# An LSTM with a feed-forward network: up to three GpSimd operations in a time step in place of two, and a new order of the work around them

## What is computed

```python
xW = einsum('ntd,dg->ntg', x, Wx) + b          # x: 32 x 64 x 256, Wx: 256 x 1024
def step(carry, xw_t):
    a = xw_t + prev_h @ Wh                     # 32 x 256 @ 256 x 1024
    i, f, o = sigmoid(...); g = tanh(a[:, 3*Hd:])
    next_c = f * prev_c + i * g
    next_h = o * tanh(next_c)
h = concatenate([hs, -hs], -1)
h = s0 * (h @ sign(k0));  h = relu(h) * 2      # to 1024 features
h = s1 * (h @ sign(k1));  h = relu(h) * 2      # 1024 x 1024
y = x + s2 * (h @ sign(k2))                    # to 256
```

## Time and profile before

| | |
|---|---|
| median of three runs | 273.42 us (273.35 to 273.68) |
| the profiled execution | 273.12 us, of which its span is 271.3 us |
| PE busy in the span | 264.2 us, 97% |
| DVE, ACT, POOL busy | 223.3, 190.7 and 83.1 us |
| chain that ended last | 80% PE, 10% DVE, 3% ACT |
| granted TensorE clock | 1.0 |

### The profile page before, as it was taken

The page is one execution under the profiler, slowest core; times in us unless marked ns, Lnnn a source line. Parts: engine busy times, 40 slices in busy tenths (PEclk is TensorE's granted clock), DMA queues, the critical chain, the costliest instruction groups (busy, mean ns, idle before and its releaser), DMA issues.

```text
span 271.3 us, 8591 instructions
## 1 busy us (share of the span) xinstructions
PE 264.2 (97%) x3360; PEld 196.1 (72%) x3360; DVE 223.3 (82%) x833; ACT 190.7 (70%) x597; POOL 83.1 (31%) x115
## 2 busy tenths in 40 slices
PE   8999999999999999899999999999999999999996
PEld 5777878888898898788988988755666544444444
DVE  3798888899898889988798999887869499993573
ACT  4798887888977778888898778888855478323220
POOL 0030200133344534533443522433422184040220
DMA  6980000000000000000000000000001010000004
GB/s 184 363 350 2 2 2 0 2 4 2 4 2 1 6 0 2 2 5 2 2 2 2 4 17 25 2 2 4 2 23 39 22 40 0 1 2 0 0 0 155
DMA packets 5288, 8.71 MB, mean 32 GB/s; under 512 B 640, under 2 KB 2944, under 8 KB 5120
## 3 DMA queue, kind: packets, MB, share of 16 engines
q1 hardware_dynamic: 4960, 7.64, 8.1%
q10 hardware_dynamic: 288, 0.52, 0.5%
HBM read 6.07 MB, written 2.10 MB: 30 GB/s over the span
## 4 chain that ended last, share of the span: by engine, by line
PE 80%; DVE 10%; ACT 3%; DMA 2%; issue 2%; POOL 1%; SPq 1%; DVEq 0%; POOLq 0%
PE WK L750 16%; PE WK L811 13%; PE WK L733 10%; PE WK L792 7%; PE GFO L712 5%; PE G L703 4%; PE G L712 4%; PE GFO L703 4%; PE ACC L834 4%; DVE aT L1346 3%; PE G L811 3%; PE GFO L852 3%; DMA xw<-in_wx 2%; PE WK L852 2%; PE WK L770 1%
## 5 line engine op out<-in xcount | busy, mean ns | idle before, releaser
L971 ACT ACTIVATE tT<-aT 128x64 f32<-128x64 f32 x189 | 44.9, 269 | 27.1 <-DVE aT L1346 19.4
L750 PE MATMUL WK<-h,k 128*128 128x256 f16 (+1 forms) x408 | 59.4, 287 | 0.1
L1346 DVE TENSOR_REDUCE aT<-GFO 128x64 f32<-128x128 f32 x128 | 36.5, 285 | 11.7 <-PE GFO L712 10.0
L750 PEld LDWEIGHTS WK<-h,k 128*128 128x128 fp8e5 x408 | 37.8, 98 | 8.8 <-ACT xw L954 0.2
L733 PE MATMUL WK<-xs,wxs 128*128 128x512 f32 x168 | 43.4, 402 | 0.0
L712 PE MATMUL GFO<-h,w 128*128 128x64 f16 x504 | 35.1, 192 | 0.0
L733 PEld LDWEIGHTS WK<-xs,wxs 128*128 128x128 f32 x168 | 30.1, 188 | 6.4 <-DVE xs L1179 0.4
L703 PEld LDWEIGHTS G<-h,w 128*128 128x128 f16 x504 | 17.8, 96 | 14.1 <-DVE h L1458 10.7
L1346 DVE TENSOR_REDUCE aT<-G 128x128 f32<-128x256 f32 x64 | 27.1, 424 | 0.0
L712 PE MATMUL G<-h,w 128*128 128x64 f16 x504 | 25.0, 193 | 0.0
L703 PE MATMUL G<-h,w 128*128 128x32 f16 x504 | 22.9, 178 | 1.7 <-DVE h L1458 1.5
(11 more groups left out here) (193 smaller groups left out, 538.8 us busy)
## 6 DMA issues: line engine op xcount, KB each, us to landing
x<-in_x SPq DMA_DIRECT2D x3, 512.0 KB, 8.1
xw<-in_wh SPq DMA_DIRECT2D x4, 256.0 KB, 5.9
k<-in_k SPq DMA_DIRECT2D x1, 1024.0 KB, 10.0
out_y<-x SPq DMA_DIRECT2D x8, 128.0 KB, 1.8
out_y<-x SPq DMA_DIRECT2D x3, 256.0 KB, 2.1
x<-in_x ACTq DMA_DIRECT2D x2, 256.0 KB, 3.6
xw<-in_wx SPq DMA_DIRECT2D x4, 128.0 KB, 4.4
xw<-in_wx SPq DMA_DIRECT2D x2, 256.0 KB, 6.1
```

The lines of the kernel that those rows point to most:

```text
L750: ins = eng.matmul(layer_src(tile), w, rhs, start=a == 0, stop=last)
L971: eng.activation(tT[:, B * j0:B * j1], aT[:, j0:j1].rearrange("p j b -> p (j b)"), ACT.Tanh, scale=half_gain0 if t == 0 else half_gain).th ...
L1346: eng.tensor_reduce(aT[:, j0:j1], G[g][:, 0:64 * (j1 - j0)].rearrange("p (j h b) -> p j b h", h=2, b=B), op=ALU.add, axis=AX.X).then_inc(a ...
```

## The change

- `CHORES` goes from 1.3 to 2.0. So POOL's list for a step can hold three operations of 0.65.
- DVE makes 16 parts of `mix` (0 to 7 and 16 to 23) and POOL 16. Such a part may now also stand in `dve[t]`, behind h.
- In place of `fresh` the planner has `late`: for each operation of ACT and POOL the time in the next step's PE work at which it is taken as done. PE's matmuls that need it, or need the PSUM bank that it frees, are put behind that point.
- A product with `mix` waits only for its own eight parts, by the semaphores `mixed0`, `mixed1` and `mixed3`.
- The first layer of chunk 4 may start with step 48, without the added delay of one step a tile.
- `ORDER` is another string.

```diff
-MIX_ORDER = tuple(range(16, 24)) + tuple(range(8, 16)) + tuple(range(24, 32))
-VECTOR_MIXES = 8
-CHORES, WINDOW, LOOK = 1.3, 1.25, 24
+MIX_ORDER = tuple(range(8, 16)) + tuple(range(24, 32))
+VECTOR_MIXES = tuple(range(8)) + tuple(range(16, 24))
+CHORES, WINDOW, LOOK = 2.0, 1.25, 24
...
+    def free_at(tile):
+
+        if tile is None:
+            return 0.0
+        ops = by_whom(tile)
+        return max(late.get(op, 0.0) for op in ops) if made.issuperset(ops) else T
...
         def have(*ops):
-            return made.issuperset(ops) and fresh.isdisjoint(ops)
+            return made.issuperset(ops) and all(late.get(op, 0.0) <= now for op in ops)
...
         elif q == 0:
-            inputs = t >= sum(CHUNKS[tile[1]]) + (tile[2] if tile[1] == N1 else 0)
+            inputs = t >= sum(CHUNKS[tile[1]])
...
-        return inputs and (old is None or emptied(old))
+        return inputs and free_at(old) <= now
...
+            now = spent if t < 0 or t > 16 else 0.9
             at = choose(t)
...
             if t == MIX_STEP:
-                to_dve += [(("mix", n), [], t) for n in range(8)]
+                to_dve += [(("mix", n), [], t) for n in VECTOR_MIXES]
...
-                if since <= t and op[0] not in pair + ("cl", "mix", "tl", "th") and (made | first).issuperset(needs) and len(dve[t]) < room:
+                if since <= t and op[0] not in pair + ("cl", "tl", "th") and (made | first).issuperset(needs) and len(dve[t]) < room:
...
-        fresh = {("P", op) for op in pool[t][1:]}
+        late = {}
+        for n, op in enumerate(act[t]):
+            late["A", op] = sum(map(act_cost, act[t][:n + 1])) - 0.9
+        for n, op in enumerate(pool[t]):
+            late["P", op] = sum(map(pool_cost, pool[t][:n + 1])) - 0.49 + 0.02 * n
...
                 elif q == 3:
-                    e.wait_ge(mixed, len(MIX_ORDER))
+                    e.wait_ge(mixed3, 8)
                     e.wait_ge(lo22S, k + 1)
                 else:
                     i = (3, 0, 1, 2)[q - 4]
-                    e.wait_ge(mixed0, VECTOR_MIXES)
-                    e.wait_ge(mixed, len(MIX_ORDER))
+                    if q in (5, 7):
+                        e.wait_ge(mixed0, 8 if q == 5 else len(VECTOR_MIXES))
+                    elif q == 6:
+                        e.wait_ge(mixed1, 8)
...
+                q, k, cols = n // 8, n % 8 // 2, slice(256 * (n % 2), 256 * (n % 2) + 256)
+                u, v, op = (a21, a22, ALU.add) if q == 0 else (a11, a21, ALU.subtract)
                 e.wait_ge(w1_made, 3)
-                eng.tensor_tensor(mix[:, 0, k, cols], a21[:, k, cols], a22[:, k, cols], ALU.add, saturate=False).then_inc(mixed0)
+                eng.tensor_tensor(mix[:, q, k, cols], u[:, k, cols], v[:, k, cols], op, saturate=False).then_inc(mixed0)
```

More of the change, by code:

```diff
@@ L190, in make_plan @@
     made = {("A", ("x", 0, j)) for j in range(NJ)}
-    fresh = set()
+    late, now = {}, 0.0
     to_act, to_dve, to_pool = [], [], []
@@ L210, in emptied @@
             ops = [("V", tile)]
-        return made.issuperset(ops)
+        return ops
     def ready(tile, a, t):
         def have(*ops):
-            return made.issuperset(ops) and fresh.isdisjoint(ops)
+            return made.issuperset(ops) and all(late.get(op, 0.0) <= now for op in ops)
         q, k = tile[0], a % 8 // 2
-        mixed = [("P", ("mix", n)) for n in MIX_ORDER]
+        mixed = {q: [("V" if n < 8 or 16 <= n < 24 else "P", ("mix", n)) for n in range(8 * i, 8 * i + 8)]
+                 for i, q in enumerate(("s5", "s6", "s7", "s3"))}
         if q == "x":
@@ L229, in ready @@
         elif q == "s3":
-            inputs = have(("V", ("l22", k)), *mixed)
+            inputs = have(("V", ("l22", k)), *mixed[q])
         elif q[0] == "s":
-            inputs = have(by("tl", {"s4": 3, "s5": 0, "s6": 1, "s7": 2}[q], k), *mixed)
+            inputs = have(by("tl", {"s4": 3, "s5": 0, "s6": 1, "s7": 2}[q], k), *mixed.get(q, ()))
         elif q in ("p1", "p2"):
@@ L254, in ready @@
         else:
-            return inputs and any(emptied(old) for _, old in free)
-        return inputs and (old is None or emptied(old))
+            return inputs and any(free_at(old) <= now for _, old in free)
+        return inputs and free_at(old) <= now
     def place(tile):
@@ L264, in place @@
         else:
-            bank[tile], before[tile] = free.pop(next((n for n, (_, old) in enumerate(free) if emptied(old)), 0))
+            bank[tile], before[tile] = free.pop(next((n for n, (_, old) in enumerate(free) if free_at(old) <= now), 0))
     def after(tile):
@@ L572, in lstm_ffn @@
         acc_mm, y_out, y_made = ([sem(f"{n}{mo}") for mo in range(2)] for n in ("acc_mm", "y_out", "y_made"))
-        mixed, mixed0, p1_made, n2_mm, r12_made, hi22, lo22 = (
-            sem(n) for n in ("mixed", "mixed0", "p1_made", "n2_mm", "r12_made", "hi22", "lo22"))
+        mixed0, mixed1, mixed3, p1_made, n2_mm, r12_made, hi22, lo22 = (
+            sem(n) for n in ("mixed0", "mixed1", "mixed3", "p1_made", "n2_mm", "r12_made", "hi22", "lo22"))
         rest_made, rest_lo = ({c: sem(f"{n}{c}") for c in (SA, N1 - 1, N1)} for n in ("rest_made", "rest_lo"))
@@ L1278, in empty @@
                 elif op[0] == "mix":
-                    mix0_part(op[1])
+                    own_mix_part(op[1])
                 elif op[0] == "t":
@@ L1522, in _ @@
                 x_hi(2, k)
-            mix_order = [op[1] for ops in pool_plan for op in ops if op[0] == "mix"]
             def mix_part(n):
                 q, k, cols = n // 8, n % 8 // 2, slice(256 * (n % 2), 256 * (n % 2) + 256)
-                u, v, op = ((mix[:, 0], a11, ALU.subtract), (a11, a21, ALU.subtract), (a12, mix[:, 1], ALU.subtract))[q - 1]
+                u, v = (mix[:, 0], a11) if q == 1 else (a12, mix[:, 1])
                 eng.wait_ge(w1_made, 3)
@@ L1532, in mix_part @@
                     eng.wait_ge(mixed0, n - 8 + 1)
-                elif q == 3:
-                    eng.wait_ge(mixed, mix_order.index(n - 16) + 1)
-                eng.tensor_tensor(mix[:, q, k, cols], u[:, k, cols], v[:, k, cols], op, saturate=False).then_inc(mixed)
+                else:
+                    eng.wait_ge(mixed1, n - 24 + 1)
+                eng.tensor_tensor(mix[:, q, k, cols], u[:, k, cols], v[:, k, cols], ALU.subtract, saturate=False).then_inc(mixed1 if q == 1 else mixed3)
             def s_term(i, k):
```

13 lines of the change are left out of this document (6 added, 7 removed).

## The result

The changed kernel takes 274.28 us in the median (273.38 to 275.02), the kernel before beside it 273.35 (272.74 to 273.78). The ratio is 1.0036, with an interval of 1.0025 to 1.0046. So it is slower, by 0.9 us. The profiled execution took 274.63 with a span of 272.8; the one of before took 273.12.

What follows compares the result with a forecast made beforehand. With 18 matmuls a step, PE's work and the chain through DVE and ACT were taken as equally long, 2.85 us. Terms -3.3 - 1.2 + 6.1 = +1.6, put on the median 273.42, gave 275.0, range 273.8 to 276.9.

Steps and rivals of the forecast that it cites:

- The two gains: Shorter steps through PE's new order and fewer waits, -3.3 us, and fewer matmuls in the tail, -1.2 us.
- What the change gives back in the steps: Steps 16 to 63: evener matmul order and fewer PE waits for POOL cut the excess from 4.47 to 1.2, -3.3.
- the twelve: Steps 14, 17 to 21, 29, 31, 33, 34, 36, 37, where POOL gets three operations; forecast 3.2 to 3.5 each.
- The tail: After h of step 63: 578 matmuls in place of 589, 11 less at 0.109, -1.2 us.
- The price of the third operation: POOL's third operation holds vT until 0.08 behind its end, in twelve steps, 0.39 to 0.65 each: +6.1 us.
- The 0.04 for the hand-over to uT and back: In each step with three POOL operations, 0.04 us allowed for passing the turn to uT and back.
- `mix` on DVE behind h pushes POOL: Steps 17, 20 and 21: a part of `mix` on DVE delays POOL's first operation, 0.2 more each.
- The bounds: Limits on the third operation's price: 5.1 with no hand-over or push, 7.3 with hand-over 0.1 and push 0.26.
- Faster, vT gets its turn at once: Rival: POOL's third operation doesn't hold the chain, as vT and cD are too short or go at once; 268.9, chance 0.13.
- No change, 0.35 a step: Rival: DVE's operations take the port ahead of POOL more often, 12 times 0.35 is 4.2, to 273.1; chance 0.07.
- Slower still: Rival: several hand-overs a step and PE readers too early, 12 times 0.7, 277.3; chance 0.10, shared with waits that stay.
- the order does nothing: Rival: PE's waits in steps 55, 59 and 61 stay (2.1), 277.1 with the holding; chance 0.10, shared with slower still.

Runs made afterwards that it cites:

- the first run: The changed kernel with CHORES back from 2.0 to 1.4, so at most two POOL operations a step, PE's and DVE's rows unchanged: 269.52 us against 272.98 before.
- both runs without the holding: The changed kernel with CHORES 1.4 (269.52 us), and the changed kernel with each third POOL operation replaced by a memset (269.1 us).
- the first two experiments: The changed kernel with CHORES 1.4 (ratio 0.9879 to the kernel before), and with a memset as third POOL operation in twelve steps (ratio 0.9867).

## Why the prediction was right, and where its terms were off

The sign, the mechanism and the size hold: 275.0 forecast, 274.28 measured, +1.6 against +0.9. In the profiled pair the sum comes nearer (+1.51) than its terms deserve. Counted as the prediction counts it, the price of the third operation is 5.4 (5.13 in eleven steps, 0.31 in step 14), 0.7 under the 6.1. The two gains were 0.15 and 0.11 short, and 0.36 at the start, which no term had, gave back the rest.

- **What the change gives back in the steps** (-3.3). The intervals outside the twelve carry an excess of 1.32 from step 16 on, where 1.2 was forecast and 4.47 stood before; so -3.15. The order without the third operation (the first run) confirms it: 135.56 for the 47 intervals, 2.86 less than before. Of the waits of the earlier trace rows 0.2 of 2.8 is left. That the parts of `mix` cost nothing alone was not quite so: by the first run they lengthen three steps by 0.15 together.
- **The tail** (-1.2): from h of step 63 to the end of DVE's last operation 59.80, 60.89 before, so -1.09.
- **The price of the third operation** (+6.1). The rule was right to 0.01 us: vT ends 0.08 to 0.09 behind POOL's end, in all twelve steps. Two additions to it were too large. The 0.04 for the hand-over to uT and back doesn't exist; POOL's third starts as if nothing had stood between, 12 x 0.04 = 0.48 less. And `mix` on DVE behind h pushes POOL by 0.11, not 0.2, in three steps, 0.27 less. That makes 6.2 - 0.75 = 5.45, while the twelve lengths are 5.5 over 12 times 2.85. And more of it covered other things than the 0.15 that I took off: against both runs without the holding it is 5.0, because the steps 14, 17, 19, 20, 21, 29 and 33 would have been 0.03 to 0.09 longer than 2.85 anyway.
- **The bounds** of this price don't follow from what they are said to hold. No hand-over and no push make 6.1 - 0.48 - 0.6 = 5.0, and 4.5 with 0.04 less again behind vT, where the prediction has 5.1. A hand-over of 0.1 and the full push make 6.1 + 0.72 + 0.18 = 7.0, where it has 7.3. The measured 5.4 lies inside either way.
- **The sum.** In the trace: -3.15 - 1.09 + 5.13 (eleven of the twelve steps; the twelfth, step 14, lies ahead of step 16) + 0.26 in the steps 0 to 15 (step 14 is 0.31 of it) + 0.36 ahead of h of step 0 = +1.51, which is 274.63 - 273.12. The 0.36 at the start was in no term; h of step 0 lies between 21.8 and 22.8 in traces of kernels that don't touch it, so I take it for no effect of the change; that it helps the profiled pair to +1.51 is luck. Of the +1.15 that remain the medians show +0.9.
- **The rivals.** "Faster, vT gets its turn at once": no step shows it, though the first two experiments landed on its number (268.9 forecast for no holding, 269.5 and 269.1 measured), as they should if the holding were the only cost. "No change, 0.35 a step": the steps paid 0.42 on the mean by the two comparisons (5.0 / 12), just above its 0.41. So that rival was nearer than its chance of 0.07 says, though not by its own reason: no step shows a DVE operation that goes ahead of POOL's third, only the two additions weren't there. "Slower still" and "the order does nothing" fall.
- What the prediction took from the Trainium skill (page SBUF — State Buffer, section SBUF: two separate sides) was half of its rule. It spoke of two inputs alone, and not of a mode in which an operation with one input is held, which no term needed here. That section also has the loser wait for the whole instruction ("the other fully blocks"), which would push POOL by the full 0.26 in three steps. The trace doesn't agree: POOL's first operation is pushed by 0.11 in each of them (it ends 1.48 behind h in place of 1.37). That is less than the 0.2 that I took, too. Step 17, whose h starts at 73.60:

```profile
74.14 0.42 DVE L1238 TENSOR_TENSOR mix<-k 128x256 fp8e5<-128x256 fp8e5 x1
...
74.30 0.79 POOL L1593 TENSOR_TENSOR h<-xw,h 128x256 f16<-128x256 f32 x1 [2.23 <-DVE h L1477]
```

## What to carry to other kernels

When DVE has a chain to keep and GpSimd has work for free places, the place ends when the chain's next operation on DVE wants to start, not when somebody wants GpSimd's result. Put the end of GpSimd's last operation of a step on a line with the operations of DVE in the chain: what overhangs costs its length, and an idle 70% of GpSimd says nothing on it. Two changes in one diff should be timed apart: here the new order with its rules gained 3.5 us alone (269.52 against 272.98), and the bigger budget lost between 4 and 5 (5.0 in the twelve steps, 4.3 by the medians' ratios). And look at all operations of DVE's chain, not only those with two inputs.

## What the runs showed of the hardware that I had not expected

- Which operation is held depends on both sides. A memset of 0.63 us left a two-input operation of DVE alone (0.23) and held a one-input tensor_scalar (0.37 in place of 0.20, to 0.05 behind its end).
- A held two-input operation of DVE of 0.22 us ends 0.08 behind the end of GpSimd's, a held tensor_scalar of 0.19 ends 0.05 behind it. In the tail of the kernel before, one of 128x512 (0.68 where nothing holds it) ended 0.55 behind the earlier trace rows. So each ends as if it had begun some 0.12 to 0.14 before GpSimd's end, an estimate from these three. In the trace the time held is in the length of the held operation (vT 304 ns in the mean in place of 224) and not in idle time with a releaser.
- Operations of GpSimd give the turn to one held operation of DVE between two of theirs (uT, at 128.13 behind 128.06) and lose no time by it: the next starts 0.05 before the end of the last all the same.
- After PE had stood for 1.81 us, the granted clock was 0.61 over the next 3.1 us, and the matmuls behind took 0.32 in place of 0.22. Behind a stop of 1.01 in the kernel before it stayed at 1.00.
- The time outside the span is 1.8 us in nearly every run, but 2.8 to 3.3 with three operations and the old order, 1.8 to 3.1 with vT of one input, and 2.2 to 3.4 with two operations and the old order. It belongs to the kernel and not to the chip, since the kernel before had 1.8 beside each. No run here isolates the cause, and it stays open.
